# Mask of the maximum pass on VectorE, stacks in 4 KB runs, a new order, tail banks and single clamps in a fused decoder layer

## The reference

```python
def _L0_xattn_ref(q, k, v, mask, Wq, Wk, Wv, Wo):
    Q = (q @ Wq.T).reshape(bsz, seq, N_HEADS, D_HEAD).transpose(0, 2, 1, 3)
    K = (k @ Wk.T).reshape(bsz, seq, N_HEADS, D_HEAD).transpose(0, 2, 1, 3)
    ...
    scores = jnp.einsum('bhqd,bhkd->bhqk', Q, K) / np.sqrt(D_HEAD).astype(np.float32)
    scores = jnp.where(mask == 0, -jnp.inf, scores)
    attn = jax.nn.softmax(scores, axis=-1)

def _act_fake_quant(x, clip_factor):
    scale = jax.nn.sigmoid(clip_factor) * jnp.max(jnp.abs(x)) / QMAX
    return jnp.clip(_ste_round(x / scale), -QMAX - 1.0, QMAX) * scale

def _L0_ffn_ref(x, clip_x, clip_down, w_gate, w_up, w_down):
    xq = _act_fake_quant(x, clip_x[0])
    gate = jnp.einsum('bsh,ih->bsi', xq, _weight_fake_quant(w_gate))
    up = jnp.einsum('bsh,ih->bsi', xq, _weight_fake_quant(w_up))
    h = _act_fake_quant(jax.nn.silu(gate) * up, clip_down[0])
    return jnp.einsum('bsi,hi->bsh', h, _weight_fake_quant(w_down))
...
    x = x + _L0_attn_ref(_layernorm(x, axis=-1), ...)
    x = x + _L0_xattn_ref(_layernorm(x, axis=-1), ctx_1024, ctx_1024, mask_1x1xSxS2_ik0, ...)
    x = x + _L0_ffn_ref(_layernorm(x, axis=-1), ...)
```

## Time and profile before

| | |
|---|---|
| median of 3 runs | 1573.05 us (1571.67 to 1575.93) |
| profiled execution, its span | 1575.61 us, 1573.8 us |
| busy in the span: PE, DVE, ACT, POOL | 1289.3 (82%), 1018.9 (65%), 780.3 (50%), 726.1 (46%) |
| mask matmuls of the maximum pass (L1359) | 256, 104.0 us, 406 ns each |
| maxima (L2016) | 256, 175.1 us, 684 ns each; idle before them 219.5 us |
| exponentials (L1618) | 256, 152.9 us, 597 ns each |
| landing of a stack load, K and Q | 5.3 us and 8.9 us (median) |

### The profile page before, as it was taken

The page is one execution under the profiler, slowest core; times in us unless marked ns, Lnnn a source line. Parts: engine busy times, 40 slices in busy tenths (PEclk is TensorE's granted clock), DMA queues, the critical chain, the costliest instruction groups (busy, mean ns, idle before and its releaser), DMA issues. The chain is left out here.

```text
span 1573.8 us, 29173 instructions
## 1 busy us (share of the span) xinstructions
PE 1289.3 (82%) x9682; PEld 902.3 (57%) x9682; DVE 1018.9 (65%) x2147; ACT 780.3 (50%) x1484; POOL 726.1 (46%) x2196
## 2 busy tenths in 40 slices
PE   4899997855588899899899899999899876863754
PEld 3667764854466666676666667667666543431233
DVE  4989886994434765676576566567566636323897
ACT  2678776113433555574465466557456422332543
POOL 2677775820244354344435445434444521014825
PEclk9999998555656999999999999999999978876878
DMA  2343433864114526545564563654454264003005
GB/s 73 115 160 123 155 129 134 176 149 158 61 51 77 125 85 105 79 110 89 85 125 93 93 115 96 105 85 110 90 85 81 55 120 57 15 27 141 0 7 180
DMA packets 182570, 154.19 MB, mean 98 GB/s; under 512 B 45822, under 2 KB 153494, under 8 KB 182422
## 3 DMA queue, kind: packets, MB, share of 16 engines
q1 hardware_dynamic: 182422, 152.34, 42.0%
HBM read 93.31 MB, written 58.72 MB: 97 GB/s over the span
## 5 line engine op out<-in xcount | busy, mean ns | idle before, releaser
L2016 DVE TENSOR_REDUCE x_maxima<-x_psA 128x2 f32<-128x512 f32 x256 | 175.1, 684 | 219.5 <-PE x_psA L1363 219.0
L1618 ACT ACTIVATE x_PT<-x_psB 128x512 f32<-128x512 f32 x256 | 152.9, 597 | 136.8 <-PE x_psB L1384 134.3
L1359 PE MATMUL x_psA<-x_mask_q,x_ident_bf 128*128 128x512 bf16 x256 | 104.0, 406 | 60.2 <-DMA x_Qs<-scratch_q_parts 51.5
L286 DVE SCALAR_TENSOR_TENSOR a_conv<-a_ps_proj,taps,a_conv 128x253 f32<-128x253 f32 (+2 forms) x288 | 115.4, 468 | 26.0 <-ACT a_conv L340 25.9
L509 PE MATMUL a_ps_proj<-a_hT,wqkv 128*128 128x256 f32 x384 | 103.0, 416 | 11.8 <-DVE a_conv L286 8.1
L1381 PE MATMUL x_psB<-x_mask_k,x_ident_bf 128*128 128x512 bf16 x256 | 101.2, 395 | 13.9 <-ACT x_PT L1618 13.7
L1363 PE MATMUL x_psA<-x_Ks,x_Qs 96*128 96x256 bf16 x512 | 103.8, 285 | 0.0
L1384 PE MATMUL x_psB<-x_Qs,x_Ks 98*128 98x256 bf16 x512 | 101.5, 280 | 0.0
L509 PEld LDWEIGHTS a_ps_proj<-a_hT,wqkv 128*128 128x128 f32 x384 | 74.8, 205 | 26.0 <-issue 9.7
L1731 POOL TENSOR_TENSOR c_og_sq<-c_og 128x2 f32<-128x2 f32 x16 | 3.1, 195 | 173.8 <-DVE c_og L1974 173.8
L1759 POOL TENSOR_SCALAR x_parts_q<-x_rest 128x512 bf16<-128x512 f32 x16 | 24.9, 1558 | 108.4 <-DVE x_rest L1994 108.4
(11 more groups left out here) (380 smaller groups left out, 3602.5 us busy)
## 6 DMA issues: line engine op xcount, KB each, us to landing
scratch_keypack<-a_keypack SPq DMA_DIRECT2D x16, 768.0 KB, 3.3
c_keypack<-scratch_keypack SPq DMA_DIRECT2D x16, 768.0 KB, 4.8
x_Ks<-scratch_k_parts SPq DMA_DIRECT2D x96, 128.0 KB, 5.3
x_Qs<-scratch_q_parts SPq DMA_DIRECT2D x96, 128.0 KB, 8.9
b_matrix<-in_long_padded SPq DMA_DIRECT2D x16, 512.0 KB, 5.9
scratch_k_parts<-x_parts_k SPq DMA_DIRECT2D x32, 192.0 KB, 5.8
scratch_q_parts<-x_parts_q SPq DMA_DIRECT2D x32, 192.0 KB, 3.5
a_x_in<-in_x SPq DMA_DIRECT2D x16, 256.0 KB, 2.8
```

Source lines behind the costliest of these rows:

```text
L286: nc.vector.scalar_tensor_tensor(acc, ps_proj[PROJ_BANK[p]][:, c, 0:L - j], taps[:, p, c, TAPS - 1 - j:TAPS - j], acc, ALU.mult, ALU.add). ...
L1359: nc.tensor.matmul(psA[:].rearrange("p t q -> p (t q)"), ident_bf[:], mask_q[:, t].rearrange("p s k -> p (s k)"), start=True, stop=False, ...
L1618: nc.scalar.activation(PT[:, k % (2 * GROUP)], psB[:], ACT.Exp, scale=XD ** -0.5).then_inc(pexp_ready, 1)
L2016: nc.vector.tensor_reduce(maxima[:, t, 2 * pair:2 * pair + 2], psA[:], AX.X, ALU.max).then_inc(maxed, 1)
```

## The change

1. **The mask of the maximum pass.** `sA` has two matmuls left, which begin the bank themselves. `mA` is now two `tensor_tensor_reduce`, one per head: each adds `mask_q` (bf16 in SBUF) to 128x256 scores in PSUM, writes the sum back into the bank, and leaves the maximum in a column of `maxima`. The mask matmul of the exp pass stays.
2. **The stacks.** The columns of the weights `wq` and `wk` are permuted (by copies on DVE at the first batch) so that a stack row is one run of 4 KB. The order of the pairs changes, so that Q takes three DMAs (48, 32 and 16 partitions) and K six: 9 issues in place of 12.
3. **The order.** A new `C_ORDER` of the same depth, with other waits on the shared banks. In a turn `sA0` to `sA2` belong to the newest batch and `sA3` to `sA15` to the one before it (before: 0 to 4 and 5 to 15); `sB0`, `sB1` to one batch and `sB2` to `sB15` to the one before it. Several operations of the delta rule and the gate move a stage ahead.
4. **Tail banks.** `sA` of the last batch alternates between `psA` and `ps_w`, `sB` of the last two batches between `psB` and `ps_u`.
5. **Biases.** The four bias matmuls of a turn are gone; the biases go into a DVE operation and into an activation that were there already.
6. **Semaphores and clip.** The clearing block between the functions is gone. POOL clears the semaphores of `phase_b` at the start of `phase_cx`. The clip constants are loaded and worked out in `phase_cx`. The FFN weights are loaded a batch earlier.
7. **Clamps of the FFN.** ACT scales `x` and adds the rounding constant (`raise_x`), one pass on POOL (DVE for block 0) clamps, ACT lowers; `xc` has two buffers. For `h`, ACT raises chunks 0 to 3 and DVE chunks 4 and 5, DVE clamps all in one pass, ACT lowers. The addition of `x2` moves from POOL to DVE.

```diff
-C_ORDER = [(0, "ld_pack"), (4, "sA5"), (5, "sB5"), (5, "eB5"), (1, "sums1a"), (1, "p1"), (1, "w5"), (4, "mA5"), (4, "sA6"),
...
+C_ORDER = [(0, "ld_pack"), (5, "sB2"), (5, "eB2"), (1, "b0"), (3, "statx"), (7, "tuh"), (1, "w0"), (5, "sB3"), (5, "eB3"),
...
-PAIRS_Q = (0, 0, 1, 0, 2, 1)
-PAIRS_K = (0, 1, 0, 2, 0, 1)
+PAIRS_Q = (0, 1, 2, 0, 1, 0)
+PAIRS_K = (0, 0, 0, 1, 1, 2)
+RUNS_Q = ((0, 0, 3), (3, 0, 2), (5, 0, 1))
+RUNS_K = tuple((r, s, 1) for r, s in enumerate(PAIRS_K))
...
+        def bank_A(b, k):
+            two = b == B - 1 and k > 0
+            return (ps_w[:].rearrange("p (t q) -> p t q", t=TT) if two and k % 2 else psA[:]), int(two)
+        def bank_B(b, k):
+            two = b >= B - 2 and k > 0
+            return (ps_u[:].rearrange("p (t q) -> p t q", t=TT) if two and k % 2 else psB[:]), int(two)
...
                     if b >= STACKS:
                         sp.wait_ge(scoreB_mm, HEAD_STEPS * (b - STACKS + 1))
                     sp.wait_ge(parts_stored[k], 32 * (b + 1))
-                    stack, pairs = (Ks[slot], PAIRS_K) if k == "k" else (Qs[slot], PAIRS_Q)
-                    for r, s in enumerate(pairs):
-                        sp.dma_start(stack[r * XD:(r + 1) * XD],
-                                     dram[k + "_parts"][b][s].rearrange("(h d) t -> d h t", d=XD)).then_inc(stack_loaded[slot], 16)
+                    stack, runs = (Ks[slot], RUNS_K) if k == "k" else (Qs[slot], RUNS_Q)
+                    rows_of = dram[k + "_parts"][b].rearrange("s p t -> (s p) t").rearrange("(c d g) t -> d c (g t)", c=FC, g=HP)
+                    for r, part_of, n in runs:
+                        sp.dma_start(stack[r * XD:(r + n) * XD].rearrange("d (c g) t -> d c (g t)", c=FC),
+                                     rows_of[part_of * XD:(part_of + n) * XD]).then_inc(stack_loaded[slot], 16)
...
                     if b + k > 0:
-                        pe.wait_ge(maxed, HEAD_STEPS * b + k)
-                    nc.tensor.matmul(psA[:].rearrange("p t q -> p (t q)"), ident_bf[:],
-                                     mask_q[:, t].rearrange("p s k -> p (s k)"), start=True, stop=False, skip_group_check=True)
+                        pe.wait_ge(maxed, HEAD_STEPS * b + k - two)
                     for s in range(2):
                         h = 2 * pair + s
-                        last = nc.tensor.matmul(psA[:, s], Qs[slot][0:S_ROWS, h, t * P:(t + 1) * P], Ks[slot][0:S_ROWS, h],
-                                                start=False, stop=True, skip_group_check=True)
+                        last = nc.tensor.matmul(bank[:, s], Qs[slot][0:S_ROWS, h, t * P:(t + 1) * P], Ks[slot][0:S_ROWS, h],
+                                                start=True, stop=True, skip_group_check=True)
...
-                    nc.vector.tensor_reduce(maxima[:, t, 2 * pair:2 * pair + 2], psA[:], AX.X, ALU.max).then_inc(maxed, 1)
+                    bank = bank_A(b, k)[0]
+                    for s in range(2):
+                        last = nc.vector.tensor_tensor_reduce(bank[:, s], bank[:, s], mask_q[:, t, s], 1.0, LOWEST, ALU.add, ALU.max,
+                                                              maxima[:, t, 2 * pair + s:2 * pair + s + 1])
+                    last.then_inc(maxed, 1)
...
-                        nc.tensor.matmul(ps_e[:, 256 + t:257 + t], og1[:, t * P:(t + 1) * P], wog2[:], start=True, stop=False)
-                        last = nc.tensor.matmul(ps_e[:, 256 + t:257 + t], ones_row[:], bog2[:], start=False, stop=True)
+                        last = nc.tensor.matmul(ps_e[:, 256 + t:257 + t], og1[:, t * P:(t + 1) * P], wog2[:], start=True, stop=True)
...
-            phase_cx(nc, sems, dram, keep, ident)
-            sems.clear()
+            phase_cx(nc, Semaphores(nc, outer), dram, keep, ident, sems_b.all)
...
+        def clamp_x(engine, queue, n):
+            queue.wait_ge(x_raised, n + 1)
+            if n == 1:
+                queue.wait_ge(xq_ready, 1)
             apart(queue)
-            engine.tensor_scalar(dst, src, top[:, 0, 3:4], QMAX, ALU.mult, ALU.min).then_inc(x_clip, 1)
-            queue.wait_ge(x_clip, 2 * n + 1)
-            apart(queue)
-            engine.tensor_scalar(dst, dst, -QMAX - 1.0, ROUND, ALU.max, ALU.add).then_inc(x_clip, 1)
+            dst = xc[n % 2][:].rearrange("p b c t -> p (b c t)")
+            engine.tensor_scalar(dst, dst, LOW, HIGH, ALU.max, ALU.min).then_inc(x_clip, 1)
...
+                nc.vector.tensor_scalar(hc[n % 2][:, RAISED:], h[:, RAISED:, n * NT:(n + 1) * NT], top[:, 1, 3:4], ROUND,
+                                        ALU.mult, ALU.add).then_inc(h_part, 1)
+                dve.wait_ge(h_raised, n + 1)
+                dve.wait_ge(h_part, n + 1)
+                nc.vector.tensor_scalar(hc[n % 2], hc[n % 2], LOW, HIGH, ALU.max, ALU.min).then_inc(h_clip, 1)
...
+                    nc.vector.tensor_tensor(y[k % (2 * TB)][:], y[k % (2 * TB)][:], x2[n % 2][:, j], ALU.add).then_inc(y_ready, 1)
```

261 lines of the change are left out of this document (143 added, 118 removed), and 31 rows, old and new, of the table C_ORDER.

## The result

The changed kernel takes 1524.47 us (median of 4 runs, 1524.02 to 1525.77) against 1573.92 us before, now a median of 4 runs too: ratio 0.9688, 95% interval 0.9671 to 0.9704. It is faster by 49 us, where 123 were forecast; the time lies above the range. The profiled span is 1523.7 us against 1573.8.

A forecast was written before the change was run, and what follows sets the result against it. PE was taken to bound the attention turns, the steps of one bank the drain. Ten turns -63, ramp -6, drain -34, gap -10, FFN -10 gave -123: 1575.6 - 123, less 2.5, about 1450 us; range 1402 to 1512.

The forecast's parts named there:

- PE's floor: Attention turns: PE's work is 46.3 us; as a rival, DVE never delays it, turn 46.5, 1403 us, chance 0.16.
- DVE's price: Maximum pass: a step with the mask on DVE takes 1.1 us, making DVE's turn 43.0 us.
- half rate: Rival, maximum pass: DVE's new operation runs at half the addition's rate, 1.7 a step; turn 55.5, 1532 us, chance 0.08.
- The coupling: Attention turns: PE loses about 4 us where sA steps wait for close-standing mA steps on DVE; turn 50.0 us.
- The clock: Attention turns: the lower clock behind the Q wait costs PE 1.5 us a turn, taken as gone.
- The loads: Q and K stacks: three fewer issues save 1.4 us; the Q wait of 3.4 us a turn goes.
- The ramp: Before the ten turns: two turns with both passes in them gain 3 us each, -6 us.
- The drain: Emptying pipeline behind the ten turns: three stretches gain 14, 12 and 8 us, -34 in all.
- the gap: Between attention stage and FFN: the clearing goes, 12.9 us becomes about 3, -10 us.
- the FFN: FFN: the gate/up half gains 5 us and the down half 5, -10 us.
- The drain's second stretch: Drain's stretch of 40.84 us: falls to 29 by a Q wait gone (6.9), masks (3) and two banks (2), -12 us.
- coupling or the load: Rival, attention turns: mA steps at 1.4 or a Q wait of some 2 us; turn 54, 1509 us, chance 0.21.

The follow-up runs named there:

- e1: Changed kernel with qlow moved behind stats on POOL, against the kernel before: 1483.39 us, ratio 0.9447.
- e13: Changed kernel with the maximum pass's mask back on PE and 12 matmuls without a use ahead of tT, against the kernel before: 1478.68 us, ratio 0.9421.
- e6: Changed kernel with 16 matmuls without a use ahead of tT, in the wait for the statistics, against the kernel before: 1467.62 us, ratio 0.9347.
- e11: Kernel before with 14 matmuls without a use ahead of the wait for the Q stack, against the kernel before: 1550.53 us, ratio 0.9897.
- e5: The changed kernel as it is, run again on another chip, against the kernel before: 1517.21 us, ratio 0.9672.
- e10: Changed kernel with 16 matmuls without a use ahead of maxT, where PE has no wait, against the kernel before: 1546.16 us, ratio 0.9899.
- e9: Changed kernel with qlow behind stats and 8 matmuls without a use ahead of tT, against the kernel before: 1498.97 us, ratio 0.9599.
- e2: Changed kernel with qlow behind stats and tT behind pv3 and sA14 on PE, against the kernel before: 1493.94 us, ratio 0.9522.
- e18: Kernel before with the mask alone on VectorE and 16 matmuls without a use in its Q wait, against the kernel before: 1557.79 us, ratio 0.9894.
- e8: Changed kernel with stacks loaded as before, 6 and 6 DMAs in 512-byte runs, no permuted weights, against the kernel before: 1533.60 us, ratio 0.9764.
- e12: Changed kernel without the tail banks, against the kernel before: 1545.17 us, ratio 0.9880.
- e3: Changed kernel with the maximum pass's mask back on PE and one maximum reduction on DVE, against the kernel before: 1497.48 us, ratio 0.9519.
- e15: Changed kernel with tT behind pv3, sA14 and vproj, p1 and ctxT between sA15 and maxT, no filler, against the kernel before: 1469.26 us, ratio 0.9367.
- e17: e15 with kproj also between maxT and logits, cTc ahead of sh1, sh2 two operations earlier, against the kernel before: 1478.74 us, ratio 0.9405.

## Why the prediction was wrong, point by point

- **PE's floor** (46.3 us a turn) came out: 46.1 in e1's turn at a clock of 1.00. The matmuls of the mask were worth 0.22 each as read from the earlier trace rows: in turns at a clock of 1.00 PE is busy for 51.66 us in e13 and 48.98 in e6, and those 2.7 us are sixteen masks less four fillers.
- **DVE's price** was too high: 0.73 a step, 38.0 a turn. The reading of the maximum hides beside the next pass (142 ns, no idle time before it). The rival at half rate did not come: 447 ns for 128x256, 0.1 us over the half of 691 for 128x512. The Trainium skill, Vector Engine (DVE) Microarchitecture Reference, "Points that are easy to get wrong", has the halving for two SBUF sources that aren't bf16; here one source is in PSUM and the other is bf16, and the 447 ns agree.
- **The coupling**, the step "PE loses about 4 us there. I take 50.0 for a turn", is the one that failed. PE does lose 4.2 us a turn, but not where I put it and not for DVE's mask. I had gone through the waits that the trace of before has and the pairs that the change touches, `sA` and `mA`. I had not gone through the chains whose cover on PE the new order shortens: PE reaches `tT` 10.5 us behind `out` (23 before), and DVE, ACT and POOL need 14.6 for what lies between, 10 of them on POOL, 2.7 of these for `qlow`, which only stands ahead in its queue. The trace of before had every duration for that. That the idle time came out near the forecast (4.9 us a turn against 3.7) is luck: it is another wait.
- **The clock** is the larger part of the error, and the term "- 1.5" in "PE's work is then 52.5 - 3.5 - 1.2 - 1.5 = 46.3" is the one that was mis-sized. I had priced the clock at 1.5 us a turn (e11 gives 2 for the kernel before) and taken it as gone with Q's wait. The new wait brought it back, and more of it: 0.89 instead of 0.95. Of the 6.0 us by which the turn missed (56.0 against 50.0), 4.8 are PE's busy time (51.1 against 46.3), which e1's 46.1 at the full clock shows to be the clock's, and 1.2 are idle time. From e5 to e6 PE was given 3.5 us more to do, and the turn fell from 55.0 to 51.05; in e11 the same was done to the kernel before. These two runs show that work in a wait of 3.4 to 4.3 us keeps the clock up behind it. The control e10 is not clean: filler outside the wait raised the clock too, from 0.89 or 0.91 to 0.93. How the clock goes with the length of a wait is not shown: e9, with 3.1 us in one wait, had 0.96, e2, with no wait over 1.7, had 0.93, and e18 had 0.87 in two turns without a wait to speak of. The Trainium skill, TensorE: Matmul & The Clock Gate, "What's actually happening", says that the throttled state is the default and activity releases it. e6 and e11 agree: with activity in the wait the clock is 1.00.
- **The loads:** the wait for Q went, but by the order and not by the runs of 4 KB (e8). The Trainium skill, DMA: Bandwidth & Descriptors, "Specifications", has 512 bytes as enough for line rate, and e8 agrees by the loads of K (4.6 us against 4.4 for the same six DMAs). Fewer issues bring Q 1.5 us sooner, and the whole of Q is there 2.2 us sooner or more; in the drain that counts.
- **The ramp** came out at +5.8 instead of -6: PE is busy for 150.5 us between 352 and the first `maxT` against 141.5, at a clock of 0.59 against 0.65 and with no more matmuls (896 against 907). The first `maxT` stands 10.5 us later than before, and two turns win 4.7 of that back, so the forecast of the two turns was near and the part ahead of them, put at nothing, was wrong. No experiment was made on it; why the clock is lower there stays open.
- **The drain, the gap and the FFN** were right within 3 us: -34.8, -10.4 and -7.4. In two of them misses cancel, which is luck. The drain's second stretch gave 8.0 instead of 12, since a wait for Q of 4.4 us stayed that I had as gone, and its third 11.9 instead of 8; its 1.72 for a step was a value at the low clock, 1.30 at the full one. The FFN's gate/up half was to give 5 us and gave 0.3, since DVE was busy for 52.0 of 60.3 us there already and POOL's relief took nothing from it, and the down half gave 6.7 instead of 5. The banks (20.7, e12) carry more of the drain than I gave them.
- The **rivals**: the half rate had the time (1532) and the turn (55.5) nearest, coupling or the load came next (1509, 54), both for reasons that did not come: steps of 1.7 or 1.4, or a Q wait. None had a third chain.
- **The mask on VectorE** in the change as it stands does not pay: without it the ratio is 0.952 (e3) against 0.967 and 0.969, though on different chips and with wide intervals. Filled, it is worth about 12 us (e13 against e6). So the runs suggest that the sign depends on the wait; each pair was run on two chips. Why e3's clock is so much better with a wait of still 2.7 us is argued only: the sixteen matmuls also are activity, and the wait is shorter.

## What to carry to other kernels

When PE bounds a pipeline in its turns and work is taken from it, go through every chain that leaves PE and comes back, sum it over the engines that it crosses from the durations at hand, and compare it with PE's work between the two ends under the new order: a chain that is longer is a new wait of PE, and the longest is the first suspect for the new bound. Price a wait of PE at its length and at what the clock costs behind it, and try a few matmuls without a use in the wait as a measurement: if the kernel gets faster (e6, e11), the clock is what is lost, and useful work should be moved there (e15). A sum that seems right should be taken apart by stretches, too: the FFN and the drain here hid two misses each. Shortening one chain by pushing an operation on a shared engine behind it only moves the wait to that operation's user (e1, e9).

## What the runs showed of the hardware

- For the same 409 matmuls in a turn the busy time was 47.5 us at a mean clock of 0.97, 50.1 at 0.91 and 53.5 at 0.85, about 1 us for each 0.02 of the clock.
- Behind a wait of 3.3 us (before) the clock was at its lower level for 3 us, behind one of 4.1 us (the change) for 13 us.
- Filler of 3.1 to 3.5 us in waits of 3.4 to 4.3 us took the clock from 0.95 to 1.00 (e11) and from 0.91 to 1.00 (e6). The same filler outside a wait: 0.93 (e10).
- Idle time in short pieces was not harmless: 3.5 to 3.8 us a turn with no wait over 1.7 us went with 0.93 (e2), 0.96 (e15) and 0.97 (e17). That it is gentler than a long wait is not shown: e9, with 3.1 us a turn in one wait, had 0.96.
- An operation on VectorE that adds, takes the maximum and writes back in PSUM took 447 ns for 128x256, and the reading of its accumulator 142 ns, hidden; a pair took 0.73 us by starts, where one maximum reduction of 128x512 took 0.68.
